# Blocked Householder tridiagonalization: one wait per instruction, halved fill-in matmuls, coefficient product behind the row products

## The reference

```python
h = jnp.maximum(_layernorm(x, axis=-1), 0.0)
x = x + _L0_gnn_ref(h, adj, ...)      # 8 Euler steps: h + dt*(alph*0.5*(adj@h - h) + h@w_eff - h + x0)
h = jnp.maximum(_layernorm(x, axis=-1), 0.0)
x = x + _L1_gnn_ref(h, adj, ...)      # L = diag(deg) - A, normalized; _, U = eigh(L); U @ mlp(U.T @ h)
h = jnp.maximum(_layernorm(x, axis=-1), 0.0)
x = x + _L2_gnn_ref(h, adj, ...)      # normalized adjacency, two linear layers with batch norm
h = jnp.maximum(_layernorm(x, axis=-1), 0.0)
x = x + _L3_gnn_ref(h, adj, ...)      # two graph products, then LSTMs over windows of 1 to 4 nodes
```

## Time and profile before

| | us |
|---|---|
| median of 3 executions | 4877.47 |
| lowest, highest | 4869.52, 4891.39 |
| profiled execution | 4896.3 |
| its span, first to last instruction | 4894.5 |
| its reflections, first to last L1484 | 98.0 to 2538.9 |

### The profile page before, as it was taken

How to read it: one execution, slowest core, us unless ns; L and a number is a source line. 1 busy time by engine, 2 the same in 40 slices (tenths; PEclk the granted TensorE clock), 3 DMA queues, 4 the chain that set the end, 5 groups by cost and what they waited for, 6 DMA issues and landing times.

```text
span 4894.5 us, 71887 instructions
## 1 busy us (share of the span) xinstructions
PE 3372.1 (69%) x20820; PEld 2043.9 (42%) x20820; DVE 3161.2 (65%) x17005; ACT 1017.9 (21%) x3735; POOL 761.4 (16%) x3360
## 2 busy tenths in 40 slices
PE   3899999899889989999970000000065857599998
PEld 2676565655565565655540000000043623244433
DVE  6657788787878877778787889999922122202333
ACT  0212222222222222222210000000012122314542
POOL 1111122222212222222222221111000000000000
PEclk7657999699879968878785555555587978689998
DMA  2000000000000000000000000000000000000000
GB/s 87 2 1 2 2 2 2 2 2 2 2 2 2 2 1 2 1 1 1 1 1 0 0 0 0 0 0 0 0 0 0 17 0 0 0 0 0 0 0 34
DMA packets 3105, 21.15 MB, mean 4 GB/s; under 512 B 432, under 2 KB 560, under 8 KB 1072
## 3 DMA queue, kind: packets, MB, share of 16 engines
q1 hardware_dynamic: 2736, 16.85, 0.9%
HBM read 12.66 MB, written 4.19 MB: 3 GB/s over the span
## 4 chain that ended last, share of the span: by engine, by line
DVE 49%; PE 42%; issue 5%; ACT 2%; POOL 1%; DVEq 1%; DMA 0%; SPq 0%; POOLq 0%; ACTq 0%
PE ps L906 6%; PE ps L624 5%; DVE H L1711 5%; PE ps L576 3%; PE ps L913 2%; DVE XYEG L1459 2%; PE ps L618 2%; DVE jq L1329 2%; DVE C L1484 2%; DVE H L1329 2%; DVE tsc L1471 2%; DVE SO L1496 2%; PE ps L661 2%; DVE tsc L1481 2%; ACT H L1092 2%
## 5 line engine op out<-in xcount | busy, mean ns | idle before, releaser
L624 PE MATMUL ps<-C 128*32 128x131 f32 (+39 forms) x10200 | 418.6, 301 | 0.0
L632 PEld LDWEIGHTS ps<-XYEG 128*128 128x128 f32 x1020 | 191.6, 224 | 380.0 <-DVE XYEG L1459 341.4
L967 POOL TENSOR_SCALAR step<-XYEG,tsc 128x8 f32<-128x8 f32 (+3 forms) x510 | 152.7, 299 | 1267.8 <-DVE tsc L1469 1267.8
L1157 ACT ACTIVATE tsc<-tsc 128x1 f32<-128x1 f32 x510 | 103.5, 203 | 1139.4 <-DVE tsc L1449 1139.4
L576 PE MATMUL ps<-C,LT 128*128 128x512 f32 x512 | 318.4, 707 | 0.0
L576 PE MATMUL ps<-WK,LT 128*128 128x512 f32 x512 | 316.0, 702 | 0.0
L1171 ACT ACTIVATE sz<-C,tsc 128x4 f32<-128x4 f32 (+3 forms) x510 | 151.7, 297 | 736.0 <-POOL C L968 736.0
L906 PE MATMUL ps<-C,V 128*128 128x512 f32 (+1 forms) x504 | 287.5, 727 | 8.5 <-issue 7.5
L618 PE MATMUL ps<-C,XYEG 128*128 128x1 f32 x1020 | 221.3, 286 | 104.1 <-DVE C L1484 83.0
L624 PEld LDWEIGHTS ps<-C 128*32 128x32 f32 x10200 | 281.8, 124 | 16.5
L645 PEld LDWEIGHTS ps<-C,XYEG 128*128 128x128 f32 x958 | 181.2, 223 | 224.1 <-POOL C L968 165.6
(11 more groups left out here) (473 smaller groups left out, 7608.3 us busy)
## 6 DMA issues: line engine op xcount, KB each, us to landing
out_x<-X SPq DMA_DIRECT2D x4, 1024.0 KB, 3.9
X<-in_x SPq DMA_DIRECT2D x2, 1280.0 KB, 20.6
X<-in_x SPq DMA_DIRECT2D x1, 1536.0 KB, 16.9
eye<-in_eye SPq DMA_DIRECT2D x1, 1026.0 KB, 9.4
WK<-in_adj SPq DMA_DIRECT2D x1, 1024.0 KB, 4.8
adjT<-in_adjT SPq DMA_DIRECT2D x1, 1024.0 KB, 6.8
WK<-in_below SPq DMA_DIRECT2D x1, 1024.0 KB, 11.0
V<-in_wih SPq DMA_DIRECT2D x1, 1024.0 KB, 5.4
```

The costliest lines, as they stand in the source:

```text
L624: m = mm(ps[q * QUAD:(q + 1) * QUAD, 0, 0:c + n], SI[:, b, 0, 2 * j:2 * j + 1].broadcast_to([P, QUAD]), AS[:, b, q, k * QUAD:P + n], start ...
L632: mm(ps[:, 1, 1:3], spread(XYEG[:, r % 2], k, 2), XYEG[:, r % 2, k, 1:4:2], start=True, stop=True).then_inc(S["pivot_ps"], 1)
L967: step(g_.tensor_scalar(step2[:, k:KB, :], this[:, :, 2:4], tsc[:, 7:8], None, ALU.mult))
```

## The change

**Waits and operations.** On PE the coefficient product goes behind the row products and has its own semaphore (`coef_ps`); `e_ready`, `zu_ready`, `y_ready` and `g_ready` are no longer waited for at those places, since another wait covers them. The value y1 comes out of a second dot product on DVE, so L632 loses a column and goes behind the sum of the dots. On DVE beta and its partner come out of one operation of two elements (`pair`), so the operation `un` goes and `sgx` comes; one operation squares the scales ahead of time (`tsc[:, 14:16]`), so that two operations with two scalings each (L1481, L1493) become plain products, and the scaling in L1491 becomes a copy, finished for all reflections at once at the end. `uz` (L1490) goes ahead of the next pivot column. The mask's wait goes to the top. On POOL the copy of x goes first. On ACT the two copies for later wait until the next reflection's root has been issued, and `PQ` has two copies, so `saved` isn't waited for any more. `near` is False: the pivot column's products stay behind the column of SO.

**Pieces.** Every piece is cut in two of 256 columns. `ROOM` says how many halves a pause takes by block: 2 and 2, 2 and 2, 2 and 1, 1 and 1. The panel update gets three pauses, behind the first transpositions, behind the second and behind the products, of `PANEL_ROOM` halves. The plan now has 1482 parts, its last in reflection 463. Its thin stretches are reflections 122 to 134, 212 to 224 and 320 to 331. `keep_clock` gives 256 columns per pause, from reflection 466 on.

```diff
-HEAT = ((512, 512),) * KB
+IDLE = 256
+ROOM = ((2, 2), (2, 2), (2, 1), (1, 1))
+PANEL_ROOM = ((1, 2, 4), (1, 2, 3), (1, 1, 1), (1, 1, 1))
...
+def pauses():
+    for p in range(PANELS):
+        for r in panel_rows(p):
+            yield (r, 0), r + 1, ROOM[r // P][0]
+            yield (r, 1), r + 1, ROOM[r // P][1]
+        if p < PANELS - 1:
+            r, k = (p + 1) * PANEL, (p + 1) * PANEL // P
+            for h in range(3):
+                yield (r, 2 + h), r, PANEL_ROOM[k][h]
...
-            g = max([self.gap] + [2 * self.seen[n] - 1 for n in needs])
-            self.tensor[g] = key + (part,)
-            self.gap = g + 1
-        return self.at(key, g // 2 + 2)
+            after = max([0] + [self.seen[n] for n in needs])
+            while self.slots[self.next][0] < (after, 1) or after > 0 and self.slots[self.next][0][0] == after and self.slots[self.next][0][1] > 1:
+                self.next += 1
+            at, root = self.slots[self.next]
+            self.tensor.setdefault(at, []).append(key + (part,))
+            self.next += 1
...
-                elif part <= KB:
-                    mb = part - 1
-                    pe.wait_ge(S["eu_sb"], t - j - 4 + mb + 1)
-                    m = mm(ps[:, bank, :], LT[:, mb, j * P:(j + 1) * P], state(k + 1)[:, :, mb, :],
+                elif part < 2 + 2 * KB:
+                    mb = (part - 2) // 2
+                    if half == 0:
+                        pe.wait_ge(S["eu_sb"], t - j - 4 + mb + 1)
+                    m = mm(some, LT[:, mb, j * P:(j + 1) * P], state(k + 1)[:, 2 * half:2 * half + 2, mb, :],
                            start=False, stop=(part == last), skip_group_check=True)
...
-                        keep_clock(HEAT[r // P][h])
...
+                pieces = PLAN.tensor.get((r, h), [])
+                if len(pieces) == 0 and r > EULER_END:
+                    pe.wait_ge(S["eu_sb"], 4 * TILES)
+                    keep_clock(IDLE)
+                for kind, i, part in pieces:
...
                 pe.wait_ge(S["x_ready"], r)
-                pe.wait_ge(S["e_ready"], r)
-                mm(ps[:, 0, c + n:c + n + 1], spread(XYEG[:, r % 2], k, 2), SI[:, k, 0, 2 * j:2 * j + 1],
-                   start=True, stop=True, skip_group_check=True)
-                if r > 1:
-                    pe.wait_ge(S["zu_ready"], r - 1)
                 for b in range(k, KB):
                     for q in range(QUADS):
                         m = mm(ps[q * QUAD:(q + 1) * QUAD, 0, 0:c + n],
                                SI[:, b, 0, 2 * j:2 * j + 1].broadcast_to([P, QUAD]), AS[:, b, q, k * QUAD:P + n],
                                start=(b == k), stop=(b == KB - 1), skip_group_check=True)
                 m.then_inc(S["row_ps"], 1)
+                mm(ps[:, 1, 0:1], spread(XYEG[:, r % 2], k, 2), SI[:, k, 0, 2 * j:2 * j + 1],
+                   start=True, stop=True).then_inc(S["coef_ps"], 1)
                 pause(r, 0)
-                pe.wait_ge(S["y_ready"], r)
-                pe.wait_ge(S["g_ready"], r)
-                mm(ps[:, 1, 1:3], spread(XYEG[:, r % 2], k, 2), XYEG[:, r % 2, k, 1:4:2], start=True, stop=True).then_inc(S["pivot_ps"], 1)
                 pe.wait_ge(S["dots_in"], r)
-                mm(ps[:, 3, 0:1], ones[:], dots[:], start=True, stop=True).then_inc(S["dots_ps"], 1)
+                mm(ps[:, 3, 0:2], ones[:], dots[:], start=True, stop=True).then_inc(S["dots_ps"], 1)
+                mm(ps[:, 1, 1:2], spread(XYEG[:, r % 2], k, 2), XYEG[:, r % 2, k, 3:4], start=True, stop=True).then_inc(S["pivot_ps"], 1)
                 pause(r, 1)
                 if (r + 1) % PANEL > 0 and r + 1 < N - 1:
...
                 if r > 1:
                     pe.wait_ge(S["zu_ready"], r - 1)
-                pe.wait_ge(S["e_ready"], r)
                 mm(ps[:, 2, 0:2 * j], spread(XYEG[:, r % 2], k, 2), SI[:, k, 0, 0:2 * j], start=True, stop=True).then_inc(S["g_ps"], 1)
...
                 m.then_inc(S["sit_ps"], 1)
+                pause((p + 1) * PANEL, 2)
                 pe.wait_ge(S["so_done"], (p + 1) * PANEL - 1)
                 for b in range(k, KB):
                     m = turn(ps[0:NS, 3, b * P:(b + 1) * P], SO[:, b, 0:NS])
                 m.then_inc(S["sot_ps"], 1)
+                pause((p + 1) * PANEL, 3)
                 pe.wait_ge(S["sit_sb"], p + 1)
                 pe.wait_ge(S["sot_sb"], p + 1)
                 for b in range(k, KB):
                     mm(ps[:, b, k * P:N], SOT[:, b * P:(b + 1) * P], SIT[:, k * P:N], start=True, stop=True)\
                         .then_inc(S["panel_ps"], 1)
+                pause((p + 1) * PANEL, 4)
...
-                fn(tsc[:, 1:2], tsc[:, 2:3], ACT.Sqrt).then_inc(S["root_ready"], 1)
+                fn(tsc[:, 2:3], tsc[:, 0:1], ACT.Sqrt).then_inc(S["root_ready"], 1)
+                if j > 0 and r > 1:
+                    keep(r - 1)
...
+                act.wait_ge(S["scale_ready"], r)
                 act.wait_ge(S["zu_ready"], r)
-                act.wait_ge(S["scale_ready"], r)
-                fn(sz[:, k:KB].unsqueeze(2), SI[:, k:KB, 0, 2 * j + 1:2 * j + 2], ACT.Copy, scale=tsc[:, 8:9])
-                fn(SO[:, k:KB, 2 * j + 1:2 * j + 2], SI[:, k:KB, 0, 2 * j:2 * j + 1], ACT.Copy, scale=tsc[:, 8:9])\
+                fn(sz[:, k:KB].unsqueeze(2), SI[:, k:KB, 0, 2 * j + 1:2 * j + 2], ACT.Copy, scale=PQ[:, r % 2, 2:3])
+                fn(SO[:, k:KB, 2 * j + 1:2 * j + 2], SI[:, k:KB, 0, 2 * j:2 * j + 1], ACT.Copy, scale=PQ[:, r % 2, 2:3])\
                     .then_inc(S["scaled"], 1)
-                fn(ES[:, r - 1, :], tsc[:, 7:9], ACT.Copy, scale=-1.0)
+                if j == PANEL - 1 or r == N - 2:
+                    keep(r)
+            def keep(r):
+                k, j = r // P, r % PANEL
+                fn(ES[:, r - 1, :], PQ[:, r % 2, 1:4], ACT.Copy, scale=-1.0)
                 fn(V[:, k:KB, r - 1:r], SI[:, k:KB, 0, 2 * j:2 * j + 1], ACT.Copy).then_inc(S["saved"], 1)
...
-                n2, x1 = ps[:, 0, c + n:c + n + 1], ps[:, 0, c + n + 1:c + n + 2]
-                xy, y1, g1 = ps[:, 3, 0:1], ps[:, 1, 1:2], ps[:, 1, 2:3]
...
+                pair, own = PQ[:, r % 2, 0:2], PQ[:, r % 2, 2:4]
+                mu, ns, nu = (PQ[:, r % 2, i:i + 1] for i in (1, 2, 3))
...
                 dve.wait_ge(S["row_ps"], r)
                 ts_(nsq, n2, 1e-33, None, ALU.add).then_inc(S["norm_ready"], 1)
+                dve.wait_ge(S["xm_ready"], r)
...
-                go(ts_(sg, x1, 0.0, -0.5, ALU.is_lt, ALU.add))
+                if near:
+                    pivot_column(r, True)
+                dve.wait_ge(S["coef_ps"], r)
+                m_sg = ch.mark(ts_(sg, x1, 0.0, -0.5, ALU.is_lt, ALU.add))
                 ch.need(m_prod)
                 v.tensor_reduce(y, terms, AX.X, ALU.add).then_inc(S["y_ready"], 1)
+                ch.need(m_sg)
+                m_sgx = ch.mark(tt(sgx, x1, sg, ALU.mult))
                 dve.wait_ge(S["root_ready"], r)
                 m_rc = ch.mark(v.reciprocal(rc, root))
                 dve.wait_ge(S["y_ready"], r)
-                ttr(jk[:, k:KB], x, y, dots[:, 0:1]).then_inc(S["dots_in"], 1)
+                if nb == 1:
+                    both = XYEG[:, r % 2, k, :].rearrange("p (t s) -> p s t", s=2)[:, 0, :]
+                    m = tt(dots[:], both, y.broadcast_to([P, 2]), ALU.mult)
+                else:
+                    go(ttr(jk[:, 0, k:KB], x, y, dots[:, 0:1]))
+                    m = ttr(jk[:, 1, k:KB], e, y, dots[:, 1:2])
+                m.then_inc(S["dots_in"], 1)
                 ch.need(m_rc)
                 m_c1 = ch.mark(stt(c1, rc, nsq, root, ALU.mult, ALU.add))
-                if r > 1:
-                    dve.wait_ge(S["saved"], r - 1)
                 ch.need(m_c1)
-                tt(mu, c1, sg, ALU.mult).then_inc(S["beta_ready"], 1)
+                stt(pair, tsc[:, 3:5], c1, tsc[:, 0:2], ALU.mult, ALU.subtract).then_inc(S["beta_ready"], 1)
                 dve.wait_ge(S["beta_ready"], r)
-                m_un = ch.mark(stt(un, x1, mu, mu, ALU.subtract, ALU.mult))
-                ch.need(m_un)
-                v.reciprocal(tsc[:, 8:10], tsc[:, 6:8]).then_inc(S["scale_ready"], 1)
+                v.reciprocal(own, pair).then_inc(S["scale_ready"], 1)
+                dve.wait_ge(S["scale_ready"], r)
+                go(tt(tsc[:, 14:16], own, ns.broadcast_to([P, 2]), ALU.mult))
+                dve.wait_ge(S["dots_ps"], r)
+                m_uy = ch.mark(stt(uy, mu, y1, xy, ALU.mult, ALU.subtract))
+                go(stt(yb, y, nu, mask, ALU.mult, ALU.mult))
                 dve.wait_ge(S["pivot_ps"], r)
                 m_tz = ch.mark(stt(tz, mu, g1, y1, ALU.mult, ALU.subtract))
-                dve.wait_ge(S["dots_ps"], r)
-                m_uy = ch.mark(stt(uy, mu, y1, xy, ALU.mult, ALU.subtract))
-                dve.wait_ge(S["scale_ready"], r)
-                m_yb = ch.mark(stt(yb, y, nu, mask, ALU.mult, ALU.mult))
                 ch.need(m_uy)
```

(13 more changed lines are left out.)

124 lines of the change are left out of this document (69 added, 55 removed).

## The result

The changed kernel takes 4692.21 us (median of 4 executions, 4676.11 to 4704.87) against 4884.43 (4 executions, 4869.52 to 4901.56) for the kernel before on the same chip: a ratio of 0.9604 with a 95% interval of 0.9558 to 0.9649. The profiled execution has a span of 4703.1 us against 4894.5, so 191.4 us less.

What follows compares the result with a forecast made beforehand. It took PE to bound turns in blocks 0 and 1 and DVE in block 2, with block 3 at PE's sum at 1.2 GHz. Terms summed to -187 us, from a median of 4877.5 to 4690 us, range 4590 to 4800.

Steps and rivals of the forecast that it cites:

- The head: DVE's chain from L1449 to the next column: gains and losses cancel, staying 2.55 us, 2.2 in block 3.
- a second wait costs some 0.07, and there are two on the head: On DVE's head, dropping two second waits saves 0.14 us per turn.
- The tail: From next column to L1449: SO starts after 0.45 us instead of 0.84; DVE's tail 0.4 less, PE's row products 0.31 sooner.
- PE now becomes the bound in blocks 0 and 1: PE's products sum to 4.1 us in block 0; with waits, turns of 4.30 and 3.78 us at 2.4 GHz.
- Panel updates: Halves in the update's gaps keep the clock up: -2.5 us each in blocks 0 and 1, -1.8 in block 2; -33 and -14.
- Low turns: Turns at 1.2 GHz and thin stretches: -14 us in block 1, +5 at block 0's end, -27 in block 2.
- Block 3: With two halves per turn, 1.2 GHz nearly throughout and turns of 3.8 us: -22 us.
- the lower neighbour: For block 3's untested density, the thin stretch's clock of 0.50 was taken over the full pauses' 1.00.
- Slower: Rival: blocks 1 and 2 stay at 1.2 GHz from reflection 122 on, about +370 us, 5060 us; chance 0.08.
- Block 2 falls and stays: Rival: block 2 falls to 1.2 GHz and stays, 4837 us, or 4870 with slow panel updates; chance 0.06.
- PE gives nothing back: Rival: turns in blocks 0 and 1 stay at 4.50 and 4.06 us, total 4795 us; chance 0.10.
- Block 3 keeps 2.4 GHz: Rival: block 3 stays at the high clock with turns of 3.05 us, 89 us more gained, 4600 us; chance 0.14.

Runs made afterwards that it cites:

- e1: Changed kernel with two halves in every pause of every block and idle products of 512 columns: 4607.58 us, ratio 0.9429.
- e9: e1 with two extra, already fulfilled waits on DVE, written ahead of the wait on the operand being made: 4631.30 us, ratio 0.9461.
- e5: e1 with two extra, already fulfilled waits on DVE, written behind the wait on the operand being made: 4617.20 us, ratio 0.9415.
- e10: e7 with the copy into drow behind the SO column, except in a panel's last reflection: 4495.99 us, ratio 0.9168.
- e11: e10 with the two waits ahead of the pivot column's products in the order of the kernel before: 4456.08 us, ratio 0.9090.
- e4: Changed kernel with the coefficient product back ahead of the row products on PE: 4761.52 us, ratio 0.9748.
- e7: e6 with the empty pauses of the first 48 reflections filled too, as far as a bank is free: 4520.04 us, ratio 0.9224.
- e2: e1 without pieces in the panel update: 4658.08 us, ratio 0.9527.
- e6: e1 with an idle product of 512 columns in empty pauses from reflection 49 on, where a bank is free: 4575.22 us, ratio 0.9348.
- e3: Kernel before with the change's halves, ROOM, PANEL_ROOM and IDLE, but its old operations, waits and PE order: 4885.81 us, ratio 0.9997.
- e8: e1 with DVE's old tail: uz behind the next column, double scalings, no two products at the end: 4720.35 us, ratio 0.9651.

## Why the prediction was right, and where it wasn't

The forecast of 4690 us stands against 4692.21. By stretch, with the terms that fall in each (the 13 updates of -33 split as 5 and 8 at -2.5 each):

| stretch | predicted | measured |
|---|---|---|
| first 47 reflections | -7 | -3.7 |
| rest of block 0 | -13 - 12.5 + 5 = -20.5 | -43.0 |
| block 1 | -25 - 20 - 14 = -59 | -59.1 |
| block 2 | -37 - 14 - 27 = -78 | -62.4 |
| block 3 | -22 | -23.1 |

The total is right because two of these miss in opposite directions by 22 and 16 us. That is luck, and so is part of the match in block 1, as the terms inside a stretch show. Predicted and measured, with each update taken together with the turn behind it, as the prediction prices it:

| stretch | turns at 2.4 GHz in both kernels | updates and the turns behind them | other turns |
|---|---|---|---|
| rest of block 0 | -13, -21.1 | -12.5, -19.0 | +5, -3.0 |
| block 1 | -25, -18.8 | -20, -22.5 | -14, -17.8 |
| block 2 | -37, -22.4 | -14, -21.1 | -27, -18.9 |

Nor do the -3.7 us of the first 47 reflections say anything about the -7: e1, which is the changed kernel in these reflections, is 10 us slower there than the changed kernel itself (318.7 against 308.6).

**The head** was to stay at 2.55 us in block 0 and, by the sums for the turn, to be 2.46, 2.37 and 2.20 in blocks 1 to 3. The medians at 2.4 GHz are 2.52, 2.42, 2.30 and 2.17 (the last from e1), against 2.62, 2.50, 2.40 and 2.29 before: 0.08 to 0.12 shorter instead of the same. The term "a second wait costs some 0.07, and there are two on the head" holds in size: e9 shows 0.07 to 0.08 for one. But it isn't the number of waits that costs, it is their order (e5 against e9, e10 against e11), and the prediction missed that the change puts such an order into the tail. The Trainium skill, "VectorE: DVE Perf Modes", section "The DRAIN you can't avoid", has it that a semaphore behind each operation costs nothing extra. No run here takes increments away, so none tests that. In the wide sense that the prediction gave it, with waits included, e5's turns agree within 0.01 us and e9's don't. The Trainium skill, "Perfetto Trace Analysis", section "Identifying Dependency Chains", notes that an instruction with several waits may get instructions of its own ahead of it for the others; it gives no price, and the price here is 0.07 to 0.11 us or nothing.

**The tail** was to have SO 0.45 us after the next column; it came at 0.55 (655.20 - 654.65), because the copy into `drow` stands ahead of it and waits for `scaled`, which comes at 0.47. The step "the dot products start 0.27 later" failed: they started 0.40 later (655.60), for the order of the waits. So the tail was 1.40, 1.18 and 1.00 us in blocks 1 to 3 (medians, the last from e1), where 1.15, 1.00 and 0.85 were predicted. The shorter head made up for a small part of it: 3.83 and 3.49 us in blocks 1 and 2 where 3.61 by DVE's sum (3.78 by PE's) and 3.37 were predicted. e10 and e11 take both misses out, and the turns become 3.63 and 3.32.

**"PE now becomes the bound in blocks 0 and 1" was wrong.** The step added PE's products to 4.1 us, and 0.1 to 0.2 for waits between them, and took 4.30 for block 0. Measured: 4.15. The turn there is a chain through both engines, next column to row products to DVE's head, in which the pieces are covered. The trace of the changed kernel shows it: reflection 49 has two halves in its pauses and reflection 65, at the same place in its panel, has four. Windows over all engines (busy time and count of PE, PEld, DVE, ACT and POOL, then the clock):

```profile
416.58:420.48 3.90, 3.04 (x46) 2.63 (x45) 3.47 (x33) 1.37 (x7) 1.05 (x5) 1.00 0.01 4
492.16:496.06 3.90, 3.90 (x51) 3.27 (x50) 3.47 (x33) 0.89 (x6) 1.05 (x5) 1.00 0.01 2
```

PE is free for 0.86 us of the first turn and busy for the whole second one, and both take 3.90 us. The prediction's sum of 4.1 us for PE was about right, then; it just wasn't what a turn waits for, and the 0.1 to 0.2 for waits between the steps didn't come on top. e4 agrees, since moving one product of 0.3 us ahead of the row products, with PE's sum unchanged, costs 0.27 us per turn. In e7 and e11, with nearly every pause filled, the medians of block 0 are 4.23 and 4.21, but over more turns; in the turns at 2.4 GHz of both kernels e7 and the changed kernel agree within 0.01 us. DVE's tail would be ready at almost the same time (its last `jq` product in block 0 starts 0.95 + 3 x 0.15 after the next column), so both had to come earlier for a gain, and e11, which shortens DVE's alone, gains nothing there. The 0.15 us too much accounts for 8 of the 22 us that the rest of block 0 gained over the forecast; of the others, 6 lie in the updates with the turns behind them and 8 in the remaining turns (granted clock 0.95 against 0.90 in the earlier trace rows).

**Panel updates.** Right in mechanism, with 3.67 us for the eight products instead of 6.92, and priced too low. In block 2 the turn with an update fell from 7.57 to 6.61 us on average, which is 1.0 and not 1.8; but the turn behind it, which the 1.8 includes, fell by 1.7 more. Over blocks 0 to 2 from reflection 48 on it is -63 us instead of -47. Not all of it comes from the pauses: e2 gives those 50 us over all blocks.

**Low turns.** In block 2 the prediction counted 20 turns at 4.90 us and 12 thin ones at 3.8. The trace has 17 at a mean of 5.1 and 12 thin ones at 3.7. What it didn't say is how the clock came back there: not in the turns, since those with three halves stayed at 1.2 GHz from reflection 333 to 351 but for a short rise at the update of 336, but at the panel update of reflection 352. The 16 us missing in block 2 are 15 in the turns at 2.4 GHz (74 of them, at 0.30 us instead of 88 at 0.42) and 8 in the other turns; the updates with the turns behind them give 7 back.

**Block 3** was right: 1.2 GHz in 112 of 119 turns, 3.85 us each. The choice of "the lower neighbour" between two rows decided it. e1 shows what the choice of the change costs, 72 us in this block. The Trainium skill, "TensorE: Matmul & The Clock Gate", section "HAM oscillation — how this bites in real kernels", asks for denser work; by e1, e6 and e7 the traces agree in direction, with 85, 32 and 55 us. That section speaks of gaps between bursts of matmuls, while block 3 lost its clock with products in every pause.

**The rivals.** "Slower" (blocks 1 and 2 stay at 1.2 GHz) didn't come: block 1 came back behind its thin stretch, and its pauses are full; in e1, where those of block 2 are full too, its turns at 1.2 GHz fall from 29 to 17. "Block 2 falls and stays" came in part, for 19 reflections, and for most of the block in e3 (87 of 120 turns). "PE gives nothing back" was the wrong question, as PE's sum didn't bound the turn; the 4795 beside it doesn't follow from its own terms either (4690 + 65 is 4755, and with the 38 on top 4793). "Block 3 keeps 2.4 GHz" was priced at 89 us for a turn of 3.05; e1, with full pauses, shows 72 for block 3 and a turn of 3.17.

**Where the time goes, by the runs.** Operations with full pauses and without the panel's: -229 us (e2); DVE's tail is worth 113 in e1 (e8) and the place of the coefficient product 69 in the changed kernel (e4). Panel pauses: -50. Thinner pauses in blocks 2 and 3: +85. What the two parts leave of the -229, some 47, is a remainder and not a measurement, since parts taken from different kernels needn't add: the pair in one operation, the dropped waits, ACT's late copies and the cut pieces are all in it, and none was tried alone.

## What to carry to other kernels

Ask of each hidden filler what it holds up besides itself: in block 3 another 512 columns of matmul per turn, whose result nobody reads from reflection 398 on, cost nothing where the clock was up (reflection 401 takes 3.06 us in e1 and 3.12 in the changed kernel, at a clock of 1.00 in both) and were worth 0.68 us of a turn through the clock. Where an engine's turn is a chain of short dependent operations, write the wait that is still open first and the fulfilled one last, and look at the gap from end to start of each dependent pair: on DVE it was 0.03 to 0.04 us here, and 0.10 to 0.15 with a wait in the wrong place. And where the clock is in play, run the parts of a change together as well as alone, since they don't add: the plan alone brought nothing (e3), the operations with full pauses 229 us (e2), and the whole change 192.

## What the runs showed of the hardware beyond that

- The order of two waits ahead of a DVE operation: 0.03 to 0.04 us from the end of the operand's producer to the start with the open wait written first (e5, the kernel before ahead of `jq`, e11), 0.10 to 0.15 with it written last (the kernel before ahead of L1484, e9, the changed kernel and e10 ahead of `jq`).
- TensorE can be busy by its records without a pause at 1.2 GHz and not come back to 2.4 for many turns. Windows of the changed kernel over all engines, four turns of block 2 and then reflections 33 to 39 (busy time and count of PE, PEld, DVE, ACT and POOL, then the clock):

```profile
1679.64:1699.98 20.34, 20.34 (x125) 17.47 (x124) 13.53 (x113) 4.00 (x21) 4.00 (x20) 0.50 0.00 1
307.17:363.57 56.40, 54.27 (x382) 45.07 (x381) 26.46 (x226) 7.49 (x39) 7.36 (x35) 0.50 0.00 1
```

  PE is busy for the whole of the first stretch and for most of the second, and the clock is 0.50 in both. With idle products in the empty pauses, and full pauses in block 2, the same reflections run at 2.4 GHz for the most part (e7).
- Two kernels with the same pieces per turn can sit at different clocks: block 2 with three halves per turn ran mostly at 2.4 GHz with turns of 3.49 us in the changed kernel (granted clock 0.86 over the block), and mostly at 1.2 GHz with turns of 5.08 us in e3 (0.62).
